# Expert activations made transposed, weights fetched tile by tile, two more shared chunks in the expert stage

## What is computed

```python
logits = flat @ router_w.T + router_bias
topk_scores, topk_idx = top_k(softmax(logits), 4)       # normalised to sum 1
h = silu(einsum('nd,ehd->neh', flat, gate_w)) * einsum('nd,ehd->neh', flat, up_w)
expert_out = einsum('neh,edh->ned', h, down_w)
out = (take(expert_out, topk_idx) * topk_scores).sum(1)
out = out + silu(flat @ sgate_w.T) * (flat @ sup_w.T) @ sdown_w.T
x = x + tanh(g_ffn) * out
```

## Time and profile before

| | us |
|---|---|
| median of 3 runs (1076.92 to 1081.31) | 1077.49 |
| the profiled execution | 1076.78 |
| its span, first to last instruction | 1074.9 |
| first load of expert rows | 590.31 |
| first load of expert results (tail) | 999.14 |

### The profile page before, as it was taken

The page is one execution under the profiler, slowest core; times in us unless marked ns, Lnnn a source line. Parts: engine busy times, 40 slices in busy tenths (PEclk is TensorE's granted clock), DMA queues, the critical chain, the costliest instruction groups (busy, mean ns, idle before and its releaser), DMA issues.

```text
span 1074.9 us, 26031 instructions
## 1 busy us (share of the span) xinstructions
PE 954.3 (89%) x6592; PEld 728.6 (68%) x6593; DVE 733.7 (68%) x2496; ACT 613.1 (57%) x2213; POOL 669.9 (62%) x935
## 2 busy tenths in 40 slices
PE   4988888988888888889769999999999999999987
PEld 2777777777777777777655666666667666776544
DVE  3788888888888988888755344444444444454696
ACT  3667766767677777767532455555555555555211
POOL 1267777777777777777662477677777677777100
PEclk9999999999999999999879899999999999999999
DMA  5511111111111111111315433333333333331794
GB/s 154 200 37 33 36 37 37 33 33 39 36 36 33 39 38 33 39 38 62 110 33 98 99 96 95 95 91 90 94 93 96 93 92 93 93 94 32 273 363 146
DMA packets 91623, 90.43 MB, mean 84 GB/s; under 512 B 21277, under 2 KB 73098, under 8 KB 91204
## 3 DMA queue, kind: packets, MB, share of 16 engines
q1 hardware_dynamic: 71876, 55.07, 18.4%
q0 software_dynamic: 17408, 33.87, 9.6%
q10 hardware_dynamic: 2304, 1.07, 0.6%
HBM read 49.72 MB, written 42.31 MB: 86 GB/s over the span
## 4 chain that ended last, share of the span: by engine, by line
PE 43%; DVE 17%; issue 16%; DMA 12%; POOL 9%; ACT 1%; POOLq 1%; SPq 0%; DVEq 0%; ACTq 0%
DMA x_rows<-payload,slot 11%; PE ps L1071 11%; POOL x_rows L432 9%; PE ps L1082 9%; DVE payload L751 3%; PE ps L1108 3%; PE ps L1066 3%; PE ps L1076 3%; PE ps L1092 3%; PE ps L1098 3%; PE ps L1035 2%; DVE kvbd L677 2%; PE ps L942 2%; DVE w_gu L881 1%; PE ps L1044 1%
## 5 line engine op out<-in xcount | busy, mean ns | idle before, releaser
L443 POOL DMA_INDIRECT y_rows<-y_sb,xin x288 | 283.0, 983 | 141.8 <-issue 80.5
L432 POOL DMA_INDIRECT x_rows<-payload,slot x256 | 251.2, 981 | 132.7 <-DVE slot L762 70.4
L836 DVE TENSOR_TENSOR h<-sg,ps 128x128 f32<-128x128 f32 x288 | 82.6, 287 | 181.6 <-ACT sg L575 181.6
L1071 PE MATMUL ps<-w_gu,xT 128*128 x576 | 175.9, 388 | 8.2 <-issue 8.2
L1082 PEld LDWEIGHTS ps<-w_dn,hT 128*128 128x128 f32 x576 | 94.4, 190 | 105.8 <-ACT hT L580 73.0
L942 PE MATMUL ps<-vt,pT 128*128 128x108 f32 x1024 | 145.6, 287 | 0.0
L580 ACT COPY hT<-ps 128x128 f32<-128x128 f32 x288 | 76.4, 265 | 109.7 <-PE ps L1076 107.4
L942 PEld LDWEIGHTS ps<-vt,pT 128*128 128x128 f32 x1024 | 130.7, 200 | 11.3 <-issue 10.9
L1082 PE MATMUL ps<-w_dn,hT 128*128 x576 | 129.9, 308 | 8.1 <-DVE y_sb L842 6.2
L575 ACT ACTIVATE sg<-ps 128x128 f32<-128x128 f32 x288 | 80.5, 280 | 72.7 <-PE ps L1071 48.8
L842 DVE TENSOR_SCALAR y_sb<-ps,xin 128x128 f32<-128x128 f32 x288 | 99.7, 346 | 24.2 <-PE ps L1082 22.5
(11 more groups left out here) (136 smaller groups left out, 1978.4 us busy)
## 6 DMA issues: line engine op xcount, KB each, us to landing
xin<-x_rows SPq DMA_DIRECT2D x288, 65.0 KB, 1.9
w_gu<-y_rows SPq DMA_DIRECT2D x16, 1024.0 KB, 8.6
y_rows<-y_sb,xin POOLq DMA_INDIRECT x288, 2.3
...
x_rows<-payload,slot POOLq DMA_INDIRECT x256, 2.4
...
```

Of the source, the lines that this page charges most:

```text
L432: nc.gpsimd.indirect_dma_start(x_rows, bass.IndirectOffsetOnAxis(ap=slot[:, v, k:k + 1], axis=0), payload[:, v, k, :], None).then_inc(sent ...
L443: nc.gpsimd.indirect_dma_start(y_rows, bass.IndirectOffsetOnAxis(ap=xin[:, u, D:D + 1].bitcast(U32), axis=0), y_sb[:, u, :], None, bounds_ ...
L836: nc.vector.tensor_tensor(h[:, u % 2, :], sg[:, u % 2, :], ps_gu[u % 2][:, H:2 * H], ALU.mult).then_inc(h_d[u % PER], 1)
L1071: after(nc.tensor.matmul(ps_gu[u % 2][:, 0:2 * H], xT[:, u % 2, :], w_gu[:, bass.ds(e * (2 * H), 2 * H)], start=True, stop=True), xT_d, n, ...
```

## The change

Gate and up are two matmuls now, with the weights as the stationary operand and the turned rows as the moving one, so the hidden activations come out already turned: `turn_h`, `h_turned` and the buffer `h` are gone. The weights of a tile's expert are loaded with its rows, 128 KB more for each tile, into a slot of `w_t`; the two loads of all experts' weights near the start are gone. Gate and up rotate over three PSUM banks (`DEEP`), and `down` and `result` of a tile come three iterations after its `gate_up`. Ten shared chunks (`MID`) run in the expert stage, four units in each of bodies 1 to 5 and 8 to 12, none in bodies 0, 6, 7 and 13 to 15; four chunks are left for the tail. Each loop pass is one body where it was two. SP reads 21 expert numbers more at the head of each body.

```diff
-MID = 8
+MID = 10
-UNIT_AT = (6, 14)
+DEEP = 3
+UNIT_AT = (1, 5, 9, 13)
...
         def bodies(body, fori):
...
-            body(0, 0, 0, first=True)
-            body(1, 0, 1)
-            with fori(1, MID - 1) as c:
-                body(2 * c, c, 0)
-                body(2 * c + 1, c, 1)
-            body(TG - 2, MID - 1, 0)
-            body(TG - 1, MID - 1, 1, last=True)
+            body(0, first=True)
+            with fori(1, 6) as j:
+                body(j, chunk=EARLY - 1)
+            with fori(6, 8) as j:
+                body(j)
+            with fori(8, 13) as j:
+                body(j, chunk=EARLY - 3)
+            with fori(13, TG - 1) as j:
+                body(j)
+            body(TG - 1, last=True)
...
             def load_tiles(j):
                 firsts = numbers(sp, tab_sb, j * TW, U3, XROWS - 128)
+                es = numbers(sp, tab_sb, j * TW + EAT, U3 + 3, E - 1)
                 for u in range(U3):
...
                     need(sp, y_sent[u], 16 * j)
+                    sp.dma_start(w_t[:, u, :], gu[:, bass.ds(es[u + 3] * (2 * H), 2 * H)]).then_inc(xin_in[u], 16)
                     sp.dma_start(xin[:, u, :], x_rows[bass.ds(firsts[u], 128), :]).then_inc(xin_in[u], 16)
...
-                nc.vector.tensor_tensor(h[:, u % 2, :], sg[:, u % 2, :], ps_gu[u % 2][:, H:2 * H],
-                                        ALU.mult).then_inc(h_d[u % PER], 1)
+                nc.vector.tensor_tensor(hT[:, u % DEEP, :], sg[:, u % DEEP, :], ps_gu[u % DEEP][:, H:2 * H],
+                                        ALU.mult).then_inc(hT_d[u % PER], 1)
...
                 for u in range(U3):
+                    if not (first and u < 3):
+                        result(n, u - 3)
                     hidden(n, u)
-                    if not (first and u < 2):
-                        result(n, u - 2)
-                    if u - 2 in UNIT_AT:
-                        mixed_hidden(c, 2 * half + UNIT_AT.index(u - 2))
-                if half:
-                    mixed_take(c)
+                    if chunk is not None and u - 1 in UNIT_AT:
+                        mixed_hidden(j + chunk, UNIT_AT.index(u - 1))
+                if chunk is not None:
+                    mixed_take(j + chunk)
...
-            def gate_up(n, u, e):
-
-                after(nc.tensor.matmul(ps_gu[u % 2][:, 0:2 * H], xT[:, u % 2, :], w_gu[:, bass.ds(e * (2 * H), 2 * H)],
-                                       start=True, stop=True), xT_d, n, u).then_inc(gu_p[u % PER], 1)
-
-            def turn_h(n, u):
-
-                after(nc.tensor.transpose(ps_hT[:, 0:128], h[:, u % 2, :], ident),
-                      h_d, n, u).then_inc(hT_p[u % PER], 1)
+            def gate_up(n, u):
+
+                after(nc.tensor.matmul(ps_gu[u % DEEP][:, 0:H], w_t[:, u % U3, 0:H], xT[:, u % 2, :],
+                                       start=True, stop=True), xT_d, n, u)
+                nc.tensor.matmul(ps_gu[u % DEEP][:, H:2 * H], w_t[:, u % U3, H:2 * H], xT[:, u % 2, :],
+                                 start=True, stop=True).then_inc(gu_p[u % PER], 1)
...
                 for u in range(U3):
-                    gate_up(n, u, es[u + 2])
-                    if u in UNIT_AT:
-                        mixed_gate(c, 2 * half + UNIT_AT.index(u))
-                    if u - 1 in UNIT_AT:
-                        mixed_up(c, 2 * half + UNIT_AT.index(u - 1))
-                    if not (first and u < 2):
-                        down(n, u - 2, es[u])
-                    if not (first and u == 0):
-                        turn_h(n, u - 1)
+                    if not (first and u < 3):
+                        down(n, u - 3, es[u])
+                    gate_up(n, u)
+                    if chunk is not None and u in UNIT_AT:
+                        mixed_gate(j + chunk, UNIT_AT.index(u))
+                    if chunk is not None and u - 1 in UNIT_AT:
+                        mixed_up(j + chunk, UNIT_AT.index(u - 1))
                     if not (last and u >= U3 - 2):
                         turn_x(n16, n, u + 2)
-                    if u - 3 in UNIT_AT:
-                        mixed_down(c, 2 * half + UNIT_AT.index(u - 3))
+                    if chunk is not None and u - 3 in UNIT_AT:
+                        mixed_down(j + chunk, UNIT_AT.index(u - 3))
```

More of the change, by code:

```diff
@@ L154, in build @@
         adj = sb("adj", [128, E])
[L155 to L156 removed]
+        past = sb("past", [128, U3 + 3, E])
+        et = sb("et", [128, U3 + 3])
         valid = sb("valid", [128, U3])
@@ L183, in build @@
         ps_p, ps_o, ps_f, ps_b = bank[4:8]
-        ps_xT, ps_gu, ps_hT, ps_dn, ps_g, ps_u, ps_y = bank[0], bank[1:3], bank[3], bank[4], bank[5], bank[6], bank[7]
+        ps_xT, ps_gu, ps_dn, ps_g, ps_u, ps_y = bank[0], bank[1:4], bank[4], bank[5], bank[6], bank[7]
         ov = ps[:, 5:7, :].rearrange("p b n -> p (b n)")[:, 0:NG * GS].rearrange("p (g c) -> p g c", c=GS)
@@ L245, in counts @@
         def counts(eng, j, last=0, dma=False):
-            per_body, each = (1, 16) if dma else (U3 // PER, 1)
+            per_body, each = (1, 32) if dma else (U3 // PER, 1)
             return [None] * dma + [each * (per_body * j + k) if isinstance(j, int) else eng.to_reg(each * (per_body * j + k))
@@ L586, in mixed_silu, with body @@
                 nc.scalar.activation(ssg[:, k % 2, :], ps_g[:, :], ACT.Silu).then_inc(ssg_d, 1)
-            def body(j, c, half, first=False, last=False):
+            def body(j, first=False, last=False, chunk=None):
                 n = counts(act, j, U3 // PER + 1)
@@ L857, in mixed_take, with body @@
                                                op0=ALU.mult, op1=ALU.add).then_inc(take_d, 4)
-            def body(j, c, half, first=False, last=False):
+            def body(j, first=False, last=False, chunk=None):
                 n = counts(dve, j, U3 // PER)
                 for u in range(U3):
+                    if not (first and u < 3):
+                        result(n, u - 3)
                     hidden(n, u)
-                    if not (first and u < 2):
-                        result(n, u - 2)
-                    if u - 2 in UNIT_AT:
-                        mixed_hidden(c, 2 * half + UNIT_AT.index(u - 2))
-                if half:
-                    mixed_take(c)
+                    if chunk is not None and u - 1 in UNIT_AT:
+                        mixed_hidden(j + chunk, UNIT_AT.index(u - 1))
+                if chunk is not None:
+                    mixed_take(j + chunk)
             bodies(body, dve.Fori)
-            for u in range(2):
-                result(counts(dve, TG), u - 2)
+            for u in range(3):
+                result(counts(dve, TG), u - 3)
             def combine(c):
@@ L1079, in down, with units @@
             def down(n, u, e):
                 tile_done(pe, y_d, n, u - 1)
-                after(nc.tensor.matmul(ps_dn[:, 0:D], hT[:, u % 2, :], w_dn[:, bass.ds(e * D, D)], start=True,
+                after(nc.tensor.matmul(ps_dn[:, 0:D], hT[:, u % DEEP, :], w_dn[:, bass.ds(e * D, D)], start=True,
                                        stop=True), hT_d, n, u).then_inc(dn_p[u % PER], 1)
-            def units(j, k):
-                unit = 4 * (EARLY + j) + k
+            def units(c, k):
+                unit = 4 * c + k
@@ L1088, in units, with mixed_gate, mixed_up @@
                 return unit if isinstance(unit, int) else pe.to_reg(unit)
-            def mixed_gate(j, k):
-                unit = units(j, k)
+            def mixed_gate(c, k):
+                unit = units(c, k)
                 nc.tensor.matmul(ps_g[:, :], w[:, W_SG + 128 * k:W_SG + 128 * (k + 1)],
-                                 x2T_all[:, bass.ds((EARLY + j) * 512, 512)], start=True,
+                                 x2T_all[:, bass.ds(c * 512, 512)], start=True,
                                  stop=True)._wait_ge(ssg_d, unit).then_inc(sg_p, 1)
-            def mixed_up(j, k):
-                unit = units(j, k)
+            def mixed_up(c, k):
+                unit = units(c, k)
@@ L1098, in mixed_up, with mixed_down @@
                 nc.tensor.matmul(ps_u[:, :], w[:, W_SU + 128 * k:W_SU + 128 * (k + 1)],
-                                 x2T_all[:, bass.ds((EARLY + j) * 512, 512)], start=True,
+                                 x2T_all[:, bass.ds(c * 512, 512)], start=True,
                                  stop=True)._wait_ge(hs_d, unit).then_inc(sg_p, 1)
-            def mixed_down(j, k):
-                unit = 4 * (EARLY + j) + k
+            def mixed_down(c, k):
+                unit = 4 * c + k
                 need(pe, hs_d, unit + 1)
```

70 lines of the change are left out of this document (29 added, 41 removed).

## The result

The changed kernel takes 1094.22 us in the median of 4 runs (1092.83 to 1097.16), the kernel before 1079.4 beside it: a ratio of 1.0136, 95% interval 1.009 to 1.0181. It is slower; 1072 was forecast. A second set of 6 runs on the chip of later experiments gave 1.0107 (1.0074 to 1.014).

The account below looks back on a forecast made before the run. TensorE bounds the mixed bodies (27.6 us), GpSimd's scatters (23.2 a body) the stage's end. Tail loads at 1010.4 + 5.6 + 51.0 + 2.8 = 1069.8, with 1.9 around the span 1072 us; range 1050 to 1094.

Parts of the forecast that it names:

- What bounds it: Expert stage: TensorE sets the pace before, GpSimd close behind; a scatter every 1.29 us, 23.2 us for 18 tiles.
- A plain tile: Expert stage, tile without shared work: set by the one bank `ps_dn`, 1.01 us.
- A plain body: Expert stage, body without units on TensorE: 18 x 1.01 plus a hand-over of 1.15, 19.3 us.
- A mixed body: Expert stage, body with four units: four cycles of 6.23, 27.6 us in all, bounds 25.6 and 28.4.
- the cycle runs without waits: Rival, mixed bodies: the product doesn't hold `result`; 25.6 instead of 27.6 a body, 20 us less, 1052; chance 0.23.
- hidden behind GpSimd, at no cost: Weights' loads on SP: 20.5 us a body, under GpSimd's 23.2; only the start comes 2.4 us later.
- The third rival: SP or the transfers set the pace in plain bodies: 26 us more, 1098, from an issue of 0.61; chance 0.13.
- The runs: Mixed bodies in two runs of five: GpSimd starves there, TensorE's lead of some 10 us ends at `xin`.
- The sum: Expert stage: bodies sum to 938.0, last scatter at 1008.1 against 996.88; the stage ends 11 us later.
- The tail: Four chunks after the stage: first `combine` 5.6 us behind its load, then 51.0 by VectorE against 64.1 before.
- The clock: Rival: TensorE's clock falls in plain bodies through short idles, 39 us or some 20 lost, 1092 to 1111; chance 0.08.
- The signs: Profile signs: mixed bodies 27 to 28 us, `hT` never waited for; wrong if clock 0.5 behind 605 us.

Follow-up runs that it names:

- e3: The changed kernel with a unit's product on VectorE one tile later, behind that tile's result; ratio 0.9983 to the kernel before.
- e1: The changed kernel without the weights' loads, SP issuing only the rows; ratio 1.0008 to the kernel before.
- e8: The changed kernel with 8 chunks in the expert stage, in two runs of four bodies with four units each; ratio 1.0145 to the kernel before.
- e2: The changed kernel with 8 chunks in the expert stage, two units in each of the 16 bodies; 1057.65 us, ratio 0.9825 to the kernel before.
- e5: The changed kernel with its 10 chunks spread over groups of three bodies (two, two, four units) behind a plain first body; ratio 0.9967 to the kernel before.
- e10: The kernel before with 10 chunks in two runs of five bodies, four units each, old tile and weights; ratio 1.0111 to the kernel before.
- e0: The changed kernel again, unedited, on the chip of the later experiments; ratio 1.0107 to the kernel before.
- e4: The changed kernel with the weights' loads on ScalarE's queue, SP issuing only the rows; ratio 1.0171 to the kernel before.

## Why the prediction was wrong

**What bounds it** held: GpSimd's step was 1.29 throughout, and a plain body on GpSimd took 23.18.

**A plain tile** was right: steps of 1.01 to 1.02 between `result`s. **A plain body** was 20.4, not 19.3: the second read of numbers in its middle (some 0.67) was left out, and the hand-over was some 1.55, between its bounds of 1.03 and 1.92. In body 6 GpSimd still set the pace (23.18), so there it only shortened TensorE's lead.

**A mixed body** was right in mechanism and short by 0.55. The product holds `result`, which starts 0.80 into the third tile where 0.69 was put (702.70 - 701.90); a cycle is 6.33 for 6.23, four times, and the rest lies in the two other tiles and the hand-over. The rival "the cycle runs without waits" was wrong for this kernel. e3 shows that the hold could be removed: without it a mixed body took 26.7, about half of the way to that rival's 25.6.

**The failed step** is "hidden behind GpSimd, at no cost", said of the weights' loads. SP's cost was nearly right (1.03 a tile for 0.96, a head of 3.6 for 3.2, so 22.2 a body for 20.5). The fault is the comparison. It was set against GpSimd's 23.2, but in bodies 0, 7 and 14 TensorE isn't held by GpSimd yet: the slots are free or come free in time, and TensorE at 20.4 eats up what SP has ahead. The text's own figures, 20.5 for SP and 19.3 for TensorE, already said so. Body 0 took 26.9 for 20.5, body 7 26.9 for 21.5, and without the loads 21.8 and 22.1 (e1): 5.1 and 4.8 us. (In body 14 the wait cost nothing: GpSimd had tiles in hand and took 23.18 for that body.) With the start (3.4 for 2.4) the fetch cost 13 us of the stage, where 2.4 were forecast. The third rival named the place but put its threshold (0.61 us an issue) against GpSimd too; the issue was 0.52, under it.

**The runs** were described in the prediction and priced about right, but as a given. Ten bodies at 28.15 on a GpSimd that needs 23.2 are 49.5 us in which it starves, and the six plain bodies can't give any of it back. Nothing was asked of the alternative. With the new tile the order costs about 3% with eight chunks (e8 1.0145, e2 0.9825) and about 1.5% with ten (changed 1.0136 and 1.0107, e5 0.9967); with the old tile, ten chunks in runs cost 1.1% against eight spread (e10). The new tile is worth 1.75% where eight chunks are spread (e2).

**The sum.** On the profile of e0, whose table was loaded 0.83 us later than before's: its span of 1087.4 is 17.6 above the 1069.8 forecast. Body 0 brought 6.6, bodies 6 and 7 together 6.3, the ten mixed bodies 2.3 (five take 139.2 and 139.1 for 138.0, the last of a run being shorter), GpSimd's last run 1.5 (it begins 3.3 behind `result`, not 1.5, and is 0.3 quicker), the tail 1.1; the table and the start 0.1 less together. They add up to 17.7. The first profile adds 5.6 of attention.

**The tail** was right: the first `combine` 5.7 us behind its load (1038.71 - 1032.98, for 5.6) and 52.1 from there to the end of the last (for 51.0).

**The clock** rival was wrong as put. Plain body 6 ran its 20 us of short idles at 1.00 (the window 772.90:793.30 above). The Trainium skill ("TensorE: Matmul & The Clock Gate", section "A second HAM failure mode: psum-queue depth-cycling") tells of a kernel whose short idles made the clock swing. Nothing in plain body 6 shows that. In this profile's expert stage the clock fell four times, each time where TensorE waited at `xin`: at the stage's start (599.8) and around the hand-over of a body (623.7, 811.4 and 995.8). It takes no `xin` for that: in e4, which has no such wait there, it fell at 790.7 behind a stop of 1.60 us at a hand-over.

**The signs.** Mixed bodies of 28, `down`s 1.28 apart behind a unit's product and the tail came close to what was named. `hT` was to be never waited for; TensorE's loads waited for it 97 times, 42.1 us in all, and whether that cost anything beside the reads of numbers isn't shown. A clock of 0.5 behind 605 us was a sign of being wrong, and it came.
